# Regrouping TensorE's list by data type, with a 32-row o-projection that takes in the expert biases, in a fused attention and mixture-of-experts kernel

## What is computed

```python
q_w, k_w, v_w, o_w = (basis @ c.T for c in (q_coeffs, k_coeffs, v_coeffs, o_coeffs))
scores = einsum(queries, keys) * decay_weights          # causal, linear: no softmax
att = einsum(scores, values) @ o_w.T * out_scale        # values have 32 columns
logits = xn @ router_w + router_b + load_balancer
rw, sel = top_k(logits, 2); rw = softmax(rw)
e0 = silu(xn @ sw_w1) * (xn @ sw_w3) @ sw_w2
e1 = gelu(sym @ me_c1w + me_c1b) @ me_c2w + me_c2b      # sym is a linear function of xn
h2 = layer_norm(syn + attn)                             # both linear in xn
e2 = layer_norm(h2 + relu(h2 @ f1w + f1b) @ f2w + f2b) @ gen_w + gen_b
e3 = gelu(xn @ ml_w1 + ml_b1) @ ml_w2 + ml_b2
out = x + att + sum of the two selected experts, weighted by rw
```

## Time and profile before

| | us |
|---|---|
| median of 3 runs | 488.86 (488.41 to 489.31) |
| the profiled execution, its own time | 489.64 |
| its span, first to last instruction | 487.8 |
| PE busy | 471.4 |
| DVE busy | 386.0 |
| ACT busy | 227.5 |
| POOL busy | 172.4 |

### The profile page before, as it was taken

How to read it: one execution, slowest core, us unless ns; L and a number is a source line. 1 busy time by engine, 2 the same in 40 slices (tenths; PEclk the granted TensorE clock), 3 DMA queues, 4 the chain that set the end, 5 groups by cost and what they waited for, 6 DMA issues and landing times.

```text
span 487.8 us, 9828 instructions
## 1 busy us (share of the span) xinstructions
PE 471.4 (97%) x3166; PEld 401.8 (82%) x3166; DVE 386.0 (79%) x1279; ACT 227.5 (47%) x455; POOL 172.4 (35%) x308
## 2 busy tenths in 40 slices
PE   3889999999999999999999999999999999999995
PEld 2769888887988889798888989888898888879884
DVE  4576978879787887978788797878879788786975
ACT  3662636436173542617355262735626373462621
POOL 4641525323252532326243232524324253331320
PEclk9789999999999999999999999999999999999999
DMA  7300010010101001010000101001010100100000
GB/s 260 15 4 22 1 45 0 1 45 1 44 0 39 4 0 43 0 43 0 23 20 0 43 0 43 0 5 38 0 43 0 43 0 0 45 0 23 2 22 22
DMA packets 18785, 11.42 MB, mean 23 GB/s; under 512 B 1136, under 2 KB 18256, under 8 KB 18768
## 3 DMA queue, kind: packets, MB, share of 16 engines
q1 hardware_dynamic: 18480, 11.20, 8.6%
q10 hardware_dynamic: 288, 0.01, 0.0%
HBM read 6.80 MB, written 4.19 MB: 23 GB/s over the span
## 4 chain that ended last, share of the span: by engine, by line
PE 94%; ACT 2%; DVE 1%; DMA 1%; issue 0%; POOL 0%; POOLq 0%; DVEq 0%
PE EX L934 23%; PE S L968 13%; PE S L969 12%; PE S L970 12%; PE EX L946 6%; PE EX L954 3%; PE ATT L1043 3%; PE S L977 2%; PE S L979 2%; PE S L978 2%; PE S L1062 2%; PE S L1061 2%; PE S L1060 2%; PE TR L1008 1%; PE TR L895 1%; PE S L1078 1%
## 5 line engine op out<-in xcount | busy, mean ns | idle before, releaser
L968 PE MATMUL S<-xh,WH 128*128 128x512 f32 x224 | 99.4, 444 | 1.7 <-ACT hid L521 1.7
L969 PE MATMUL S<-xl,WH 128*128 128x512 f32 x224 | 89.0, 397 | 0.0
L970 PE MATMUL S<-xh,WL 128*128 128x512 f32 x224 | 88.9, 397 | 0.0
L432 POOL TENSOR_TENSOR hidl<-hid,hidh 128x512 fp32r<-128x512 f32 x32 | 40.6, 1293 | 80.1 <-ACT hidh L544 80.1
L934 PEld LDWEIGHTS EX<-W,hid 128*128 128x128 f32 x512 | 59.6, 191 | 1.4
L934 PE MATMUL EX<-scaled,hid 128*128 128x128 f32 x512 | 59.8, 275 | 0.0
L934 PE MATMUL EX<-W,hid 128*128 128x128 f32 x512 | 59.7, 274 | 0.0
L934 PEld LDWEIGHTS EX<-scaled,hid 128*128 128x128 f32 x512 | 58.5, 192 | 0.1
L968 PEld LDWEIGHTS S<-xh,WH 128*128 128x128 f32 x224 | 42.4, 189 | 18.8 <-issue 3.6
L684 DVE SCALAR_TENSOR_TENSOR OUT<-EX,coef,OUT 128x128 f32<-128x128 f32 x192 | 53.8, 343 | 1.3 <-PE EX L946 0.2
L759 DVE SCALAR_TENSOR_TENSOR gate<-th,S 128x512 f32<-128x512 f32 x64 | 43.9, 686 | 12.3 <-ACT th L507 11.6
(11 more groups left out here) (169 smaller groups left out, 938.0 us busy)
## 6 DMA issues: line engine op xcount, KB each, us to landing
X<-x SPq DMA_DIRECT2D x16, 256.0 KB, 3.0
out<-OUT SPq DMA_DIRECT2D x16, 256.0 KB, 2.4
W<-weights SPq DMA_DIRECT2D x1, 768.0 KB, 8.1
W<-weights SPq DMA_DIRECT2D x1, 512.0 KB, 5.7
W<-weights SPq DMA_DIRECT2D x1, 384.5 KB, 6.7
W<-weights SPq DMA_DIRECT2D x1, 384.0 KB, 6.2
W<-weights SPq DMA_DIRECT2D x1, 192.5 KB, 4.5
W<-weights SPq DMA_DIRECT2D x1, 162.0 KB, 4.4
```

The lines of the kernel that those rows point to most:

```text
L432: pool.tensor_tensor(hidl[:, j, :], hid[2][:, j, :], hidh[:, j, :], ALU.subtract) \
L968: pe.matmul(bank[:, :], wh, hi, start=True, stop=False)
L969: pe.matmul(bank[:, :], wh, lo, start=False, stop=False)
L970: pe.matmul(bank[:, :], wl, hi, start=False, stop=True).then_inc(unit_ready, 1)
```

## The change

`UNITS` and PE's list are reordered: the fp32 work (scores, transpose, st, experts 1 and 2 of the group before, attention) stands together, then all of f1, a1 b1, m0 m1, a2 b2, a3 b3 and f2 in fp32r, then all the fp32 work to the end of the turn. The o-projection becomes four products of 32 rows and 128 columns, each at its own partition group and into its own S bank (new units at0 to at3). The biases of experts 1, 2 and 3 become four more such products, of transposed routing weights `coefT` by a matrix `biases` made in setup; four fp32 products with 32 output rows transpose `coef`, and ACT copies them. The ones product (L930), the DVE steps L694 (scale and bias of expert 2) and L839 (bias of expert 1) go; expert 2 is mixed with coef times rstd. DVE's, ACT's, POOL's and SP's lists follow in a new order. The diff, cut to its core:

```diff
-UNITS = ([f"tok{t}" for t in range(NT)] + ["a0", "b0", "c0", "c1", "c2", "c3"]
-         + ["sc", "st", "a1", "b1", "f1_0", "f1_1", "a2", "b2", "a3", "b3", "f2", "m0", "m1", "ut"])
+UNITS = ([f"tok{t}" for t in range(NT)] + ["a0", "b0", "c0", "c1", "c2", "c3", "sc", "st", "f1_0", "f1_1", "a1", "b1",
+                                           "m0", "m1", "a2", "b2", "a3", "b3", "f2"] + [f"at{t}" for t in range(NT)] + ["ut"])
...
+        selected = sb("selected", [P, C])
+        biases = sb("biases", [P, P])
...
-        coef = [sb(f"coef{k}", [P, NT, E]) for k in range(2)]
+        coef = [sb(f"coef{k}", [P, NT, C]) for k in range(2)]
+        coefT = sb("coefT", [NT * C, P])
+        coef_r = sb("coef_r", [P, NT])
...
-        back = sb("back", [NT * C, T])
+        back = sb("back", [NT * C, P])
...
             def turn(g, first, last):
+                if two_more(g):
+                    sp.wait_ge(ex_taken, g.count(MIXES, 1))
+                    load_x(Group(g.pair, g.off + 2))
                 if not first:
                     store(g.prev())
-                if two_more(g):
-                    sp.wait_ge(att_added, g.count(1, 1))
-                    load_x(Group(g.pair, g.off + 2))
...
                     root_u(g.prev())
                 if first:
                     low_weights(range(FIRST_SPLITS, len(WEIGHT_SPLITS)))
-                    norm_x(g.next())
-                pool.wait_ge(hid_high, g.count(1, 1))
                 for j in range(2):
+                    pool.wait_ge(hid_high, g.count(2, j + 1))
                     pool.tensor_tensor(hidl[:, j, :], hid[2][:, j, :], hidh[:, j, :], ALU.subtract) \
                         .then_inc(hid_low, 1)
-                if two_more(g):
-                    norm_x(Group(g.pair, g.off + 2))
+                if not last:
+                    norm_x(g.next())
...
-                            act.copy(back[t * C:(t + 1) * C, t * P:(t + 1) * P], oT[:, :]).then_inc(back_laid, 1)
+                            act.copy(back[t * C:(t + 1) * C, :], oT[:, :]).then_inc(back_laid, 1)
...
-                half_gate(1)
                 st, free = unit("st")
                 act.copy(state[:, :], st[0:BEHIND * C, 0:C]).then_inc(free, 1)
+                for j in range(2):
+                    f, free = unit(f"f1_{j}")
+                    act.activation(hid[2][:, j, :], f[:, :], ACT.Relu, bias=vec(f"f1b{j}")).then_inc(free, 1)
+                half_gate(1)
+                for j in range(2):
+                    act.wait_ge(released[g.bank(f"f1_{j}")], g.uses_before(f"f1_{j}") + 1)
+                    act.copy(hidh[:, j, :], hid[2][:, j, :]).then_inc(hid_high, 1)
+                act.wait_ge(lean_ready, g.count(1, 1))
+                act.activation(tlean[:, :, :], lean[:, :, :], ACT.Tanh).then_inc(tlean_ready, 1)
                 act.wait_ge(found_ready, g.count(1, 1))
                 act.copy(found[:, :], ATT[:, 0, :]).then_inc(found_taken, 1)
                 for j in range(2):
-                    f, free = unit(f"f1_{j}")
-                    act.activation(hid[2][:, j, :], f[:, :], ACT.Relu, bias=vec(f"f1b{j}")).then_inc(free, 1)
-                act.wait_ge(released[g.bank("f1_1")], g.uses_before("f1_1") + 1)
-                act.copy(hidh[:, :, :], hid[2][:, :, :]).then_inc(hid_high, 1)
-                act.wait_ge(lean_ready, g.count(1, 1))
-                act.activation(tlean[:, :, :], lean[:, :, :], ACT.Tanh).then_inc(tlean_ready, 1)
+                    m, free = unit(f"m{j}")
+                    act.activation(hid[1][:, j, :], m[:, :], ACT.Gelu, bias=me_b[:, j:j + 1]).then_inc(free, 1)
                 half_gate(2)
                 half_gate(3)
+                act.wait_ge(coef_turned, g.count(1, 1))
+                act.copy(coefT[:, :], ATT[:, 1, :]).then_inc(coef_taken, 1)
                 if not last:
                     take_x(g.next())
-                for j in range(2):
-                    m, free = unit(f"m{j}")
-                    act.activation(hid[1][:, j, :], m[:, :], ACT.Gelu, bias=me_b[:, j:j + 1]).then_inc(free, 1)
...
+                dve.wait_ge(pool_const, POOL_CONSTS)
+                link(dve.tensor_reduce(selected[:, :], ident[:, :].rearrange("p (t c) -> p c t", c=C), AX.X, ALU.add))
+                link(dve.tensor_scalar(biases[:, :], prod("ml_b"), selected[:, 3:4], None, ALU.mult))
+                link(dve.scalar_tensor_tensor(out=biases[:, :], in0=gen_bias[:, :], scalar=selected[:, 2:3],
+                                              in1=biases[:, :], op0=ALU.mult, op1=ALU.add))
+                took(dve.scalar_tensor_tensor(out=biases[:, :], in0=row("me_c2b"), scalar=selected[:, 1:2],
+                                              in1=biases[:, :], op0=ALU.mult, op1=ALU.add))
...
+            def expert2(g):
...
                 dve.wait_ge(u_rstd, g.count(1, 1))
+                dve.tensor_tensor(coef_r[:, :], coef[g.par][:, :, 2], rstd["u"][:, :], ALU.mult).then_inc(scaled_r, 1)
+                dve.wait_ge(scaled_r, g.count(1, 1))
+                dve.wait_ge(ex_taken, g.count(MIXES, 3))
                 dve.wait_ge(ex_ready, g.count(E, 4))
                 for t in range(NT):
-                    ins = dve.scalar_tensor_tensor(out=e2[:, t, :], in0=EX[EX_BANK[2]][:, t, :],
-                                                   scalar=rstd["u"][:, t:t + 1], in1=gen_bias[:, :],
-                                                   op0=ALU.mult, op1=ALU.add)
-                ins.then_inc(ex_taken, 1)
-
-            def expert1(g):
-                dve.wait_ge(ex_taken, g.count(E, 2))
-                mix(g, 3, 1)
-
-            def expert2_add(g):
-                dve.wait_ge(ex_taken, g.count(E, 4))
-                for t in range(NT):
-                    ins = dve.scalar_tensor_tensor(out=OUT[g.par][:, t, :], in0=e2[:, t, :],
-                                                   scalar=coef[g.par][:, t, 2:3], in1=OUT[g.par][:, t, :],
+                    ins = dve.scalar_tensor_tensor(out=OUT[g.par][:, t, :], in0=EX[EX_BANK[2]][:, t, :],
+                                                   scalar=coef_r[:, t:t + 1], in1=OUT[g.par][:, t, :],
                                                    op0=ALU.mult, op1=ALU.add)
                 ins.then_inc(out_ready, 1)
...
                 dve.tensor_tensor(qd[:, :], qk_bank[0:BEHIND * C, 0:BEHIND * P], reach[:, :], ALU.mult) \
                     .then_inc(qd_ready, 1)
+                if not first:
+                    u_combine(g.prev())
                 masked_scores()
                 if first:
                     fold_first()
                 if not first:
                     expert0(g.prev())
-                    u_combine(g.prev())
                 dve.wait_ge(h2_high, g.count(1, 1))
                 dve.tensor_tensor(h2l[:, :], h2[:, :], h2h[:, :], ALU.subtract).then_inc(h2_low, 1)
-                silu(1)
...
-                silu(2)
+                    fold_last()
+                silu(1)
+                if not last:
+                    x_moments(g.next())
                 dve.wait_ge(tlean_ready, g.count(1, 1))
-                route(dve.scalar_tensor_tensor(out=coef[g.par][:, :, :], in0=tlean[:, :, :], scalar=1.0,
+                route(dve.scalar_tensor_tensor(out=coef[g.par][:, :, 0:E], in0=tlean[:, :, :], scalar=1.0,
                                                in1=half[:, :, :], op0=ALU.add, op1=ALU.mult))
                 assert rs[0] == ROUTE_STEPS
+                silu(2)
+                if not first:
+                    expert1(g.prev())
                 silu(3)
...
                 f2, free = unit("f2")
                 dve.scalar_tensor_tensor(out=u[:, :], in0=f2[:, :], scalar=vec("f2b"), in1=h2[:, :],
                                          op0=ALU.add, op1=ALU.add).then_inc(free, 1)
...
+                if not first:
+                    expert2(g.prev())
+
+                wait(dve, out_stored[g.par], g.half(DMA_INC, 0))
+                for t in range(NT):
+                    at, free = unit(f"at{t}")
+                    dve.tensor_tensor(OUT[g.par][:, t, :], at[:, 0:P], X[g.par][:, t, :], ALU.add).then_inc(free, 1)
+                for t in range(NT):
+                    b = g.bank(f"at{t}")
+                    dve.wait_ge(released[b], g.uses_before(f"at{t}") + 1)
+                mix(g, 1, 3)
                 if not last:
                     x_low(g.next())
...
-                if e == 3:
-                    pe.matmul(EX[EX_BANK[3]][:, :, :].rearrange("p t n -> p (t n)"), ones[:, :], b2_rows[:, :],
-                              start=True, stop=False)
                 for t in range(NT):
                     for j in range(4):
                         ins = pe.matmul(EX[EX_BANK[e]][:, t, :], hid[e][:, j, t * P:(t + 1) * P],
-                                        weight[:, j * P:(j + 1) * P], start=(e == 0 and j == 0),
-                                        stop=(j == 3 and (e == 0 or t == NT - 1)))
```

(50 more changed lines are left out.)

69 lines of the change are left out of this document (15 added, 54 removed).

## The result

The changed kernel takes 494.96 us (median of four runs, 494.17 to 495.58) where the kernel before takes 488.86 (four runs, 488.41 to 489.31): ratio 1.0124, interval 1.0106 to 1.0141. It is slower by 1.2%. The profiled execution took 494.79 itself, its span is 493.0 where that of before is 487.8.

What follows compares the result with a forecast made beforehand. PE was taken to bound the kernel. Per turn -0.27 us on PE plus 0.1 of waits, times 16, plus 0.7 first turn, minus 1.0 tail, gave -3.0: median 486.0 us, range 478 to 495.

Steps and rivals of the forecast that it cites:

- The direction: Whole kernel: the change makes it faster, by 3.0 us; chance of faster 0.53.
- a small surcharge stands wherever the kind of product changes: PE, fp32/fp32r borders at expert 3, expert 0 and attention to f1: regrouping saves 0.16 + 0.15 + 0.13 us per turn.
- The saved part: PE, per turn: removing L1043 saves 0.85 us and removing the ones product L930 saves 0.23.
- The coef block: PE, four transposes of coef: 0.24 us plus 0.17 to enter and 0.12 to leave, 0.53 per turn added.
- The at block: PE, at0 to at3: row groups run side by side, two rounds 0.43 us, with entry and exit 0.72 per turn.
- Rival 1: At block: weight loads of the four row groups go one by one, 1.99 us instead of 0.72; total 506, chance 0.22.
- Rival 2: DVE delivers silu(2) and expert 1 late; PE waits 0.5 us per turn at f2 and expert 3; 492.4, chance 0.12.
- Rival 3: New tiled blocks pay no drains at entry and exit, costing 0.64 us together; total 476, chance 0.1.
- Rival 4: Surcharges at changes of product kind hang on semaphore waits and stay: +7 us on the forecast, 493; chance 0.08.
- The first turn: Once only: a1 and b1 no longer fill PE's idle time before f1; taken +0.7 us, bounds -0.1 and +2.
- The tail: End of kernel: one of two DVE passes over expert 2 goes, coef_r comes: -1.0 us.

Runs made afterwards that it cites:

- run 3: Changed kernel's order, but o-projection and expert biases as before (no tiled blocks), and DVE's moments of x ahead of silu(1): 495.92 us, ratio 1.0115 to the kernel before.
- run 9: Kernel before in its order, only the o-projection tiled, ones product out, DVE adding biases of experts 1 and 3: 490.03 us against 489.11, ratio 1.0017.
- run 5: Changed kernel with DVE's moments of the next x moved ahead of silu(1): 493.89 us, ratio 1.0092 to the kernel before.
- run 2: Changed kernel's order of all lists, but o-projection and expert biases done as before, so neither tiled block: 497.02 us, ratio 1.0149 to the kernel before.
- run 4: Changed kernel without the four products transposing coef and ACT's copy of them, coefT zero: 491.33 us, ratio 1.0038 to the kernel before.
- run 1: Kernel before with expert 0's output cut into four pieces, m0 and m1 products between them, adding type switches: 490.13 us against 489.74, ratio 1.0007.
- Run 7: Changed kernel with ACT's once-only first-turn work moved later, behind the copy of state and the last gate pair: 492.12 us, ratio 1.0068 to the kernel before.
- run 10: Kernel before with only the o-projection tiled, ACT's once-only work later, and next xn's transposes moved into the middle of expert 0's output: 482.71 us, ratio 0.9844.
- run 6: Changed kernel with a1 and b1 back in front of f1, their tanh and silu moved along: 509.06 us, ratio 1.0400 to the kernel before.
- run 8: Kernel before with ACT's once-only work moved later, back copied behind state, the rest behind the relus: 487.14 us against 489.11, ratio 0.9945.

## Why the prediction was wrong

- **The direction.** On record stood -3.0 us, measured in the span are +5.2. The gap of 8.2 is 6.1 in the 14 middle turns (0.44 each), 2.0 in the first turn, and 0.15 at the end. The median of 494.96 lies 0.04 inside the stated 478 to 495, in the part that was there for the rivals; that is no merit of the sum.
- **The step that failed first: "a small surcharge stands wherever the kind of product changes"**, 0.16 + 0.15 + 0.13 per turn. The first two were remainders: a stretch less 16 x 0.213 for fp32 products, from "about 3.4" for sixteen, where the rows have 3.49 from 267.15 to 270.64, and even that is 0.08 short. With 0.2235 sixteen are 3.58, and 3.80 - 3.58 - 0.23 is nothing. The third was a cost, but not one of the data type: of the 1.23 us from 260.87 to 262.10, 0.10 is left at the right price, the second half of leaving attention's form. The kernel after pays it as well, now on f1's first product, 0.34 from 264.71 to 265.05 where 0.23 is due. Against the same rows the check was open, and the text noticed one switch without a surcharge ("the switch to fp32r behind it cost nothing"). By the ledger above the stretches concerned gave 0.13 together (-0.17 with 0.19 of wait and block inside it, against +0.23), of which about 0.1 is a shorter spacing of the fp32r products (see the last section), and by run 3 about 0.02. So 0.3 to 0.4 per turn was missing; that alone, 5 to 6 us, turns the sign.
- **The saved part was right**: 0.85 + 0.23 = 1.08 of L1043 and L930, both out of the list.
- **The coef block was right in its sum, by luck**: 0.355 for four transposes to the next start, 0.09 in and 0.10 out: 0.545, on record 0.53. Its entry had been taken too high (0.17, from a remainder with the same 0.213), and its way out too low (0.12, where 0.10 more falls on the next product); the two errors cancel. The rule of the Trainium skill that was weighed (TensorEngine Tiling (Array Packing), Key Properties: a change of tiling mode drains the engine) agrees with the trace: time is lost on both sides of every such block, and run 9 shows it again (0.20 in expert 0's output around the round).
- **The at block was nearly right**: 0.80 for 0.72. That the four row groups run side by side was right; each round costs 0.22 by itself, as the sum had it. What was too small are the borders: 0.29 was taken, and 0.36 are there. They stand in part inside the two rounds, which is why these read 0.33 and 0.33 from start to start (the last section has the rows).
- **Rival 1** (weight loads one by one, 506, chance 0.22) is refuted. This is the timeline of the loads of the kernel after:

```profile
277.42 0.31 PEld L1056 LDWEIGHTS S<-back,found 32*128 32x128 f32 x8
277.64 0.32 PEld L1059 LDWEIGHTS S<-biases,coefT 32*128 32x128 f32 x8
```

Eight loads of 128 columns stand within 0.31 us, where one alone is 0.19, and the second eight within 0.32. Loads of all 128 rows start 0.112 apart, so eight of them would need 0.97: loads into different row groups run side by side. By loads one after another the block would have been 1.99. The Trainium skill has both rules (TensorE: Matmul & The Clock Gate, LDWEIGHTS: a load goes by its columns; Part 2: a load is pulled ahead of running products where the row groups don't conflict, or where it goes into the background buffer); the trace agrees with the second, as the loads of the second round start at 277.64 under the first round's products, and the rival had weighed the first alone.
- **Rival 2** (DVE late, 492.4, chance 0.12) was right in its mechanism and small in size: 0.1 per turn at f2, which run 5 takes away (0.14). In runs 2, 3 and 4 the same lateness at expert 1's mix is 0.2 to 0.3 per turn, and in the kernel after the coef block lies over it. So a part of what was booked as the block's cost was also DVE's slack.
- **Rival 3** (drains not paid) is refuted by the borders above.
- **Rival 4** named 493 and was nearest. It said that the surcharges would stay, and gave as its sign the one row that did not fit them. Its cause, waits on semaphores, is not what runs 1 and 3 show: two of the three surcharges were only a product's price taken 5% too low, and the third is the way out of attention's form.
- **The first turn** was taken at +0.7 of bounds -0.1 and +2, and is +2.5: outside. The step "PE idles till h2l, 29.18" was right in kind (h2l came at 29.80); what it missed is how long PE would now stand still in front of f1: 3.52 us against 1.71 before, since a1 and b1 no longer fill the wait. h2l, at the end of a chain through ACT's once-only copies, also came 0.6 later than taken. The low clock, to which it gave a part of the +0.7, lasts as long as before. Run 7 gives 2.7 us back by moving ACT's work.
- **The tail** came out at the -1.0 on record, and one of DVE's two passes over expert 2's output is gone from it; with the -0.17 of the last turn the record had -1.2.

## What to carry to other kernels

Take the price of an instruction from the pitch of its records in a long even stretch and put it back into every other stretch before you call a remainder a cost: an error of 5% in a price that stands sixteen times looks like a surcharge at each border. A block taken off a bound engine is worth its length only up to the next producer that it covered (here 0.23 of 0.545, and less than nothing of 0.45 in run 9), so look for who is late next and move its consumer too: in run 10 the same products, with ACT's once-only work moved, became a gain of 1.6%. And read the first pass of a pipelined loop by itself: once-only work in the middle of an engine's queue cost both kernels some 2 to 3 us. Two traces can differ by 1 us there through the granted clock alone, so judge such an edit by the runs, or by the idle time.

## What the runs showed that was not expected

- Four fp32 products of 32 rows and 128 columns in four row groups cost what a single product of 128 rows costs, 0.22 us, once TensorE is in that form. Every fp32 product is two records, so a round is two passes of four. Windows cut behind the first and the third pass show where the second and the fourth start, in the PE timeline of the kernel after:

```profile
277.64 0.29 PE L1056 MATMUL S<-back,found 32*128 32x128 f32 x4
...
277.86 0.29 PE L1059 MATMUL S<-biases,coefT 32*128 32x128 f32 x4
```

The four passes start at 277.42, 277.64, 277.75 and 277.86, and the transposes at 278.08: steps of 0.21, 0.11, 0.11 and 0.22, where records of full products stand 0.112 apart. So only the first and the last step are too long, by 0.1 each; with 0.09 in front of the block and 0.06 behind it these are its borders, 0.36 us in all. Two rounds share them, which a single round cannot: alone in the list it takes 0.43 from start to start (runs 9 and 10), with more lost around it. The Trainium skill gives a speedup of 3.07 for four row tiles of 512 columns (TensorE: Matmul & The Clock Gate, Measured speedup vs the span model); no run here has that form.
- In a long unbroken run of fp32r products of 512 columns they can stand 0.227 us apart: in the kernel after 15 steps take 3.41 us (268.06 to 271.47). In the kernel before 11 steps take 2.57 (264.35 to 266.92), 0.2335 each. Runs 4 to 7, made from the kernel after, have the shorter spacing in a part of each turn, and runs 1 to 3 and 8 to 10 do not. It holds for about half of the 36 products, so it is worth some 0.1 us per turn, and it sits inside the -0.17 of the ledger.
  Run 3 has the same order of these products and the longer spacing, and run 10 has tiled blocks and the longer spacing, so neither alone is the cause. What the cause is was not tried, and stays open; it also means that "regrouping is worth 0.02" holds for the spacing of run 3, and that in the kernel after the 0.1 may belong to the edits that runs 2 and 3 leave out.

Not tried is the change as it stands with both of its cures (the edits of runs 5 and 7) at once. By their differences, 2.0 to 2.8 us in the first turn and 14 x 0.14 = 2.0 in the others, it would be 4 to 5 us under after, and so still 1 to 2 us above the kernel before; this is an estimate from runs 5 and 7.
